# The output phase of an attention layer: where the sync engine packs a chunk's softmax denominators

## The chip, the cores and the metric

The kernel runs on one core of one Trainium2 chip. The metric is the device time of one execution in microseconds (us). The kernel before was timed three times: median 5889.22 us, from 5888.39 to 5891.15.

## The reference

The program is one layer of a convolution-like two-dimensional recurrence, one layer of Nystrom attention and one recurrent feed-forward layer over 16 images of 64 x 64 positions with 128 channels, all in float32. The change lies in the attention layer (8 heads of 16 channels, 64 landmarks), in the part that turns queries into outputs:

```
sim1  = einsum('bhid,bhjd->bhij', q, k_l)       # 4096 queries x 64 landmarks, per head
attn1 = softmax(sim1, axis=-1)
out   = attn1 @ attn2_inv @ (attn3 @ v)          # attn2_inv @ (attn3 @ v) is a small matrix, computed earlier
out   = out + conv1d(v, conv_w)                  # 33 taps along the tokens, per head
out   = x + (out @ w_out + b_out)
```

The result plus the residual is then normalised over the channels of each token and goes to the feed-forward layer.

## The kernel before

The program runs phase after phase: group norm, recurrence, landmarks, pseudo-inverse, output, feed-forward recurrence. The change touches only the output phase, `output_phase`. It works through 16 images (b) of 8 chunks (c) of 512 tokens, so 128 chunks. Every engine has its own program, a loop over the chunks whose body is called `slot(b, c, ...)`; the order in a slot is written out by hand, and semaphores tie the engines together. The engines work on different chunks in one slot (a software pipeline).

What happens to a chunk c:
- TensorE computes its queries (L2138), the maxima's products (L2152), the scores (L2171, L2175), and in `weigh` (L2185) the unnormalised output. ScalarE exponentiates (L2318) and copies the two halves of the heads to the tiles `even` (L2310) and `odd` (L2312); this counts the semaphore `denc`. Each tile holds four heads: of 32 partitions, 16 hold the unnormalised outputs of one head, and the other 16 its softmax denominators, 16 times the same row.
- The sync engine (SP), which here does nothing but issue DMAs, packs the denominators of the 8 heads, one row of 512 each, into the small tile `den_packed` with all 128 partitions in use: `pack(b, c)`, two DMAs from SBUF to SBUF (L1987).
- VectorE merges the halves (`merge`, L2391), waits for the packed denominators and takes their reciprocals (`reciprocals`, L2386), one slot after the chunk's own.
- SP writes the reciprocals to the DRAM scratch `recips` (`spread`, two DMAs, L1996; it waits for the reciprocals, and at L1994 until the broadcast before it has landed, since there is one `recips` for all chunks), and reads them back 16 times each to the tile `rden` (`broadcast`, one DMA of 256 KB, L2003; it waits for the spread to have landed).
- VectorE, a slot later still, waits for `rden`, multiplies (`normalise`, L2397) and adds the convolution (`add_convolved`, L2380, which writes `oT`). TensorE projects `oT` with w_out (`project`, L2211). VectorE adds the residual and takes the statistics (L2366, L2369, L2372), GpSimd (POOL) scales (L2082 to L2089) and SP stores (`store_scaled`, L1978).

So in its slot c VectorE does, in this order: maxima of chunk c+1, residual of c-3, merge and reciprocals of c-1, normalise and add of c-2. SP's slot c is, in this order: store of c-4, load of the base tile c+1 (L1547, waits for the residual of c-3), spread of c-1, the loads of the values `v` (two DMAs of 272 KB, L1553, for the next or next but one image; there are none in the second half of image 14 and in image 15), broadcast of c-1, pack of c, load of the tokens c+6 (L1544). All of them go out on one hardware queue, which is spread over the 16 DMA engines. The values are used by the convolution in TensorE's slot (`convolve`, L2197), which waits for four slots' worth of them at once, at every fourth slot.

Of the kernel before, what the change touches and what calls it, by code (L numbers as in the profile page):

```python
# [1877 lines left out]
def output_phase(nc, sems, R, E, K, xnt, tokens, vals, recips, scaled):  # L1878


    with ExitStack() as ctx:
# [47 lines left out]
        def nth(b, c):  # L1929

            return NG * b + c + 1

        def wait(eng, name, count):

            if count > 0:
                eng.wait_ge(s[name], count)
# [5 lines left out]
        def each_image(eng, slot):  # L1942

            def image(b, q, first, last):
                for c in range(NG):
                    slot(b, c, q, first, last)
            for b in range(B):
                image(b, b % 2, b == 0, b == B - 1)

        def follows(c, k, last):  # L1950

            return c + k < NG or not last

        def precedes(c, k, first):

            return c >= k or not first

        def at(b, c):

            return (b, c) if 0 <= c < NG else (b + c // NG, c % NG)  # L1960
# [3 lines left out]
        @block.sync  # L1964
        def _(sp):
            def load_tokens(b, c):
                E.load_tokens(sp, xnt, b, c)

            def load_base(b, c):
                E.load_base(sp, tokens, b, c)  # L1970

            def load_v(b, half, piece):
                E.load_v(sp, vals, b, half, piece)

            def store_scaled(b, c):
                wait(sp, "u", nth(b, c))
                b0, c0 = at(b, c)
                sp.dma_start(scaled[b0, 512 * c0:512 * c0 + 512, :].rearrange("(n p) c -> p n c", p=P), u[c % 2][:, :, 1:1 + C]  # L1978
                             ).then_inc(s_ust[c % 2], 16)

            def pack(b, c):

                wait(sp, "denc", 2 * nth(b, c))
                wait(sp, "rec", nth(b, c) - 1)
                for h, tile in enumerate((even[c % 2], odd[c % 2])):
                    row = DH * (1 - h)
                    sp.dma_start(den_packed[LM * h:LM * h + LM, :], tile[row:C:QUAD, :].rearrange("g (j e) -> g j e", j=DH)  # L1987
                                 ).then_inc(s_packed, 16)

            def spread(b, c):  # L1990

                wait(sp, "rec", nth(b, c))
                if nth(b, c) > 1:
                    sp.wait_ge(s_rden, 16 * (nth(b, c) - 1))  # L1994
                for h in range(2):
                    sp.dma_start(recips.rearrange("(g a) (j e) -> a g j e", a=2, j=DH)[h], rec_packed[LM * h:LM * h + LM, :]  # L1996
                                 ).then_inc(s_spread, 16)

            def broadcast(b, c):

                sp.wait_ge(s_spread, 32 * nth(b, c))
                wait(sp, "att", nth(b, c) - 2)
                sp.dma_start(rden[c % 2][:, :], recips.unsqueeze(1).broadcast_to([HEADS, DH, 512])).then_inc(s_rden, 16)  # L2003

            def slot(b, c, q, first, last):
                if precedes(c, 4, first):
                    store_scaled(b, c - 4)
                if precedes(c, 3, first) and follows(c, 1, last):
                    wait(sp, "res", nth(b, c - 3))
                    load_base(*at(b, c + 1))  # L2010
                if precedes(c, 1, first):
                    spread(b, c - 1)

                if c < GT and b + 1 < B:
                    wait(sp, "conv", NG * (b + 1))
                    load_v(b + 1, 1, c)
                if c >= GT and b + 2 < B:
                    wait(sp, "conv", NG * (b + 1) + GT)
                    load_v(b + 2, 0, c - GT)
                if precedes(c, 1, first):  # L2020
                    broadcast(b, c - 1)
                pack(b, c)
                if follows(c, 6, last):

                    wait(sp, "qm", nth(b, c + 2))
                    load_tokens(*at(b, c + 6))
            wait(sp, "conv", GT)
            for piece in range(GT):
                load_v(1, 0, piece)
            for c in range(4, 6):  # L2030
                wait(sp, "qm", c - 3)
                load_tokens(0, c)

            each_image(sp, slot)
            spread(B - 1, NG - 1)
            broadcast(B - 1, NG - 1)
            for c in range(NG - 4, NG):
                store_scaled(B - 1, c)
            for q in range(2):
                sp.wait_ge(s_ust[q], 16 * B * NG // 2)  # L2040
# [817 lines left out]
```

## Time and profile before

| | |
|---|---|
| median of three runs | 5889.22 us |
| the profiled execution, its time | 5894.68 us |
| the profiled execution, its span | 5892.9 us |
| mean granted TensorE clock | 0.981 of full speed |
| output phase within the span | about 2520 to 3568 us |
| TensorE busy over the whole span | 89% |
| VectorE, ScalarE, GpSimd busy | 52%, 53%, 26% |

The profile is one execution. Its rows come from several views: groups of busy time, waits (who waited for whom), the timeline (each instruction with its start and its length), and stretches (busy time of each engine between two times). For a DMA, a timeline row is its *issue* on SP's queue, not its transfer; when it landed shows only in what was waiting for it.

### The profile page before, as it was taken

Reading aid. Unit: us, or ns where it says so; the run is one execution under the profiler, and the core shown is the slowest. Engines: PE = TensorE matmul, PEld = TensorE weight load, DVE = VectorE, ACT = ScalarE, POOL = GpSimd, SP = SyncE. Lnnn points to the kernel's source line nnn. Section 1 sums busy time; section 2 is a strip of 40 time slices with the busy share of each in tenths; the row PEclk is TensorE's granted clock in tenths of the full one; section 3 lists DMA queues with packets and bytes.
Section 4 is the critical chain, followed back from the end, with each engine's and each line's share of the span. In section 5 each row is a group of like instructions: output and inputs, shape, how many; then the busy total and the mean of one; then the engine's idle time right before and its main releaser. Section 6 shows DMA issues by size and latency. Waiting matters only on the chain. (4 is left out here: it accounts for less than half of the span.)

```text
span 5892.9 us, 223296 instructions
## 1 busy us (share of the span) xinstructions
PE 5223.6 (89%) x97395; PEld 3271.2 (56%) x97488; DVE 3058.7 (52%) x8152; ACT 3136.4 (53%) x9108; POOL 1516.7 (26%) x1905
## 2 busy tenths in 40 slices
PE   5599999997899888799999997888888888888888
PEld 4599888896566666645555443333333333333333
DVE  8677777775888886568888882111111111111111
ACT  6455555564677776478888883333333333333333
POOL 2100000001888875246666661000000000000000
PEclk7899999999999999999999998999999999999999
DMA  9631111225887773457777762111111111111100
GB/s 389 272 116 58 58 58 58 73 77 183 253 246 236 238 243 116 103 162 207 207 208 207 204 175 66 32 32 32 34 33 32 32 33 34 32 32 32 35 18 24
DMA packets 773031, 689.32 MB, mean 117 GB/s; under 512 B 67056, under 2 KB 663024, under 8 KB 767984
## 3 DMA queue, kind: packets, MB, share of 16 engines
q1 hardware_dynamic: 754672, 575.39, 32.8%
q0 software_dynamic: 14672, 95.16, 4.0%
q8 instruction: 743, 12.17, 0.9%
q10 hardware_dynamic: 2736, 4.89, 0.2%
q14 instruction: 208, 1.70, 0.1%
HBM read 392.17 MB, written 274.89 MB: 113 GB/s over the span
## 5 line engine op out<-in xcount | busy, mean ns | idle before, releaser
L2796 ACT ACTIVATE f_y<-f_acc 128x16 f32<-128x16 f32 x4096 | 753.8, 184 | 1541.3 <-PE f_acc L2738 1541.3
L2738 PEld LDWEIGHTS f_acc<-f_y,f_vT 128*32 128x32 f32 x32768 | 644.8, 108 | 1436.7 <-ACT f_y L2796 1436.1
L2738 PE MATMUL f_acc<-f_y,f_vT 128*32 128x16 f32 x32768 | 1045.7, 193 | 278.1 <-issue 0.4
L2696 PE MATMUL f_junk<-f_idle 128*32 128x512 bf16 x8400 | 831.9, 376 | 0.0
L2578 DVE COPY f_zT<-f_zt 128x512 f32<-128x512 f32 x124 | 85.8, 692 | 1136.6 <-PE f_zt L2652 1136.6
L2355 DVE TENSOR_REDUCE o_m<-o_bank_l 128x8 bf16<-128x512 f32 x512 | 328.8, 683 | 98.7 <-PE o_bank_l L2152 98.7
L2571 DVE TENSOR_SCALAR f_wxn<-f_wxp,f_scale,f_shift 128x512 f32<-128x512 f32 x126 | 102.0, 810 | 508.8 <-PE f_wxp L2666 508.8
L1299 ACT ACTIVATE a_p<-a_s 128x512 f32<-128x512 f32 x502 | 259.2, 602 | 153.6 <-PE a_s L1166 151.7
L533 POOL DMA_DIRECT2D hidden<-l_h x46 | 34.6, 754 | 1162.8 <-DVE l_hsum L790 961.5
L712 ACT ACTIVATE l_gate<-l_pf,r_ctx 128x256 f32<-128x256 f32 (+7 forms) x512 | 202.4, 446 | 229.8 <-PE l_pf L643 229.6
L2318 ACT ACTIVATE o_p<-o_bank_s 128x512 f32<-128x512 f32 x512 | 264.4, 602 | 101.2 <-PE o_bank_s L2175 101.2
L2591 DVE SCALAR_TENSOR_TENSOR f_sum<-f_u,f_std,f_turned 128x128 f32<-128x128 f32 x512 | 143.4, 342 | 317.9 <-PE f_turned L2689 317.9
L2696 PEld LDWEIGHTS f_junk<-f_idle 128*32 128x32 bf16 x8400 | 249.9, 99 | 0.0
L1359 DVE TENSOR_REDUCE a_m3p<-a_s 128x1 f32<-128x512 f32 x360 | 223.4, 682 | 50.0 <-PE a_s L1126 48.5
L633 PE MATMUL l_pio<-l_x,r_k_lm 128*128 128x256 f32 (+7 forms) x1024 | 239.0, 356 | 0.2 <-ACT l_gate L729 0.2
L633 PE MATMUL l_pf<-l_x,r_k_lm 128*128 128x256 f32 (+7 forms) x1024 | 238.9, 356 | 0.0
L647 PE MATMUL l_pio<-l_hsum,r_ctx 128*128 128x256 f32 (+7 forms) x1024 | 238.8, 356 | 0.0
L2302 ACT ACTIVATE o_base<-o_base,r_loss,r_gain 128x128 f32<-128x128 f32 x512 | 225.4, 497 | 0.0
L2689 PE MATMUL f_turned<-f_ident,f_y 128*32 128x128 f32 x4096 | 221.3, 290 | 0.5 <-DVE f_sum L2591 0.5
L1017 POOL TENSOR_TENSOR a_r<-a_vare,a_half 128x8 f32<-128x8 f32 x128 | 209.7, 1639 | 10.0
L712 ACT ACTIVATE l_gate<-l_pio,r_ctx 128x256 f32<-128x256 f32 (+7 forms) x512 | 203.3, 450 | 14.0
L2678 PE MATMUL f_acc<-f_wxn,f_ident 128*32 128x128 f32 x4096 | 207.1, 274 | 0.8 <-issue 0.8
(323 smaller groups left out, 11466.4 us busy)
## 6 DMA issues: line engine op xcount, KB each, us to landing
o_v<-vals SPq DMA_DIRECT2D x256, 272.0 KB
a_hid<-hidden SPq DMA_DIRECT2D x112, 520.0 KB, 5.0
hidden<-l_h POOLq DMA_DIRECT2D x46, 1040.0 KB, 6.8
l_x<-skew SPq DMA_DIRECT2D x46, 1024.0 KB, 5.2
vals<-a_v SPq DMA_DIRECT2D x128, 272.0 KB, 3.6
gn_x<-in_x SPq DMA_DIRECT2D x16, 2048.0 KB, 18.0
a_xin<-in_x SPq DMA_DIRECT2D x128, 256.0 KB, 4.9
tokens<-a_t SPq DMA_DIRECT2D x128, 256.0 KB, 3.4
```

The costliest lines, as they stand in the source:

```text
L633: mm = nc.tensor.matmul(banks[c][g][:, :, rows], w[W[g]], xs, start=g in (0, 2, 3), stop=False, skip_group_check=True)
L647: mm = nc.tensor.matmul(banks[c][g][:, :, rows], w[U[g]], hsum[:, lanes[c], rows], start=False, stop=True, skip_group_check=True)
L712: nc.scalar.activation(gate[:, g, lanes[c], rows], banks[c][g][:, :, rows], ACT.Tanh if g == 2 else ACT.Sigmoid, bias=bias[BI[g]]).then_in ...
L1299: nc.scalar.activation(p3[c % 2][g][:, :], score_bank(i, c, g), ACT.Exp).then_inc(s["exp"], 1)
L1359: nc.vector.tensor_reduce(m3p[:, g, c:c + 1], bank[:, :], AX.X, ALU.max).then_inc(s["mx"], 1)
L2302: nc.scalar.activation(bs[c % 4][:, k, :], bs[c % 4][:, k, :], ACT.Identity, scale=R.gain[:, b, n:n + 1], bias=R.loss[:, b, n:n + 1]).then ...
L2318: nc.scalar.activation(p1[g][:, :], bank_s[g][:, :], ACT.Exp).then_inc(s["exp"], 1)
L2355: nc.vector.tensor_reduce(m1[:, 2 * r:2 * r + 2, LM * half:LM * half + LM].rearrange("p k (g r) -> p k g r", r=QUAD)[:, :, :, 0:2], bank_l ...
L2689: mt = nc.tensor.matmul(turned[g % 2][rows, b % 4, :], y[q][:, rows, b], ident[:, :], start=True, stop=True)
L2696: nc.tensor.matmul(junk[rows, :], idle[:, 0:QUAD], idle[:, :], start=True, stop=True)
L2738: mm = nc.tensor.matmul(acc[k % 2][rows, t, :], vT[:, rows], before, start=False, stop=True, skip_group_check=True)
L2796: nc.scalar.activation(y[q][:, step, :], acc[step // RC % 2][:, step % RC, :], ACT.Sigmoid).then_inc(s_y, 1)
```

## The change

One line moves in SP's slot: `pack(b, c)` now stands directly behind `spread(b, c - 1)`, before the loads of v and before `broadcast(b, c - 1)`.

```diff
@@ -2010,7 +2010,7 @@
                     load_base(*at(b, c + 1))
                 if precedes(c, 1, first):
                     spread(b, c - 1)
-
+                pack(b, c)
                 if c < GT and b + 1 < B:
                     wait(sp, "conv", NG * (b + 1))
                     load_v(b + 1, 1, c)
@@ -2019,7 +2019,6 @@
                     load_v(b + 2, 0, c - GT)
                 if precedes(c, 1, first):
                     broadcast(b, c - 1)
-                pack(b, c)
                 if follows(c, 6, last):
 
                     wait(sp, "qm", nth(b, c + 2))
```

In the body of the phase, SP's instructions of one slot stand like this in the kernel before (recips<-o_rec_packed is the spread, o_v<-vals the values, o_rden<-recips the broadcast, o_den_packed the pack, o_xnT the tokens, scaled<-o_u the store, o_base<-tokens the base tile):

```order
L1996 DMA recips<-o_rec_packed 4x16x32 x2
L1553 DMA o_v<-vals 128x4x136 x2
L2003 DMA o_rden<-recips 128x1x512
L1987 DMA o_den_packed<-o_even 64x1x32
L1987 DMA o_den_packed<-o_odd 64x1x32
L1544 DMA o_xnT<-xnt 128x512
L1978 DMA scaled<-o_u 128x4x128
L1547 DMA o_base<-tokens 128x4x128
```

The same slot in the changed kernel:

```order
L1996 DMA recips<-o_rec_packed 4x16x32 x2
L1987 DMA o_den_packed<-o_even 64x1x32
L1987 DMA o_den_packed<-o_odd 64x1x32
L1553 DMA o_v<-vals 128x4x136 x2
L2003 DMA o_rden<-recips 128x1x512
L1544 DMA o_xnT<-xnt 128x512
L1978 DMA scaled<-o_u 128x4x128
L1547 DMA o_base<-tokens 128x4x128
```

The two small DMAs of the pack have moved ahead of three large ones, and the two values loads and the broadcast have each moved two instructions back. In the last image and a half, where no values are loaded, SP's slot in the changed kernel is:

```order
L1996 DMA recips<-o_rec_packed 4x16x32 x2
L1987 DMA o_den_packed<-o_even 64x1x32
L1987 DMA o_den_packed<-o_odd 64x1x32
L2003 DMA o_rden<-recips 128x1x512
L1544 DMA o_xnT<-xnt 128x512
L1978 DMA scaled<-o_u 128x4x128
L1547 DMA o_base<-tokens 128x4x128
```

There the pack and the broadcast have changed places. The other engines' programs are the same.

## Rows read from the trace of the kernel before

**Rows 1.** Busy time by stretch, output phase while values are still loaded.

```profile
core 0: us, PE busy (x) PEld busy (x) DVE busy (x) ACT busy (x) POOL busy (x), PEclk, DMA share, GB/s
2571.00:3462.00 891.00, 855.33 (x10454) 445.34 (x10454) 739.53 (x1889) 751.25 (x1558) 604.01 (x613) 1.00 0.74 207
```

**Rows 2.** One line of the kernel, L2386 (the reciprocals), same stretch.

```profile
L2386 DVE RECIPROCAL o_rec_packed<-o_den_packed x112: 342/353/355, 2571.5 to 3461.6; 128x32 f32<-128x32 f32 x112
```

**Rows 3.** Waits, same stretch, TensorE: in total us, times, longest.

```profile
PE o_bank_x L2211 <- DVE o_oT L2380: 23.3, 27, 2.4
PE o_bank_s L2197 <- DMA o_v<-vals: 6.8, 8, 1.3
```

**Rows 4.** Waits, same stretch, VectorE.

```profile
DVE o_rec_packed L2386 <- DMA o_den_packed<-o_odd: 56.5, 80, 1.8
DVE o_att L2397 <- DMA o_rden<-recips: 4.7, 6, 1.2
```

**Rows 5.** Waits, same stretch, SP's queue.

```profile
SPq L1994 <- DMA o_rden<-recips: 100.3, 93, 2.1
SPq L1996 <- DVE o_rec_packed L2386: 69.2, 99, 1.8
SPq L2003 <- DMA recips<-o_rec_packed: 11.0, 22, 1.4
```

**Rows 6.** Timeline of SP over one slot: start, length, DMA issued.

```profile
3011.47 1.14 SPq L1996 DMA_DIRECT2D recips<-o_rec_packed  x2
3012.66 1.01 SPq L1553 DMA_DIRECT2D o_v<-vals  x2
3013.85 0.63 SPq L2003 DMA_DIRECT2D o_rden<-recips  x1
3014.58 0.56 SPq L1987 DMA_DIRECT2D o_den_packed<-o_even  x1
3015.19 0.54 SPq L1987 DMA_DIRECT2D o_den_packed<-o_odd  x1
3015.78 0.45 SPq L1544 DMA_DIRECT2D o_xnT<-xnt  x1
...
3019.56 1.15 SPq L1996 DMA_DIRECT2D recips<-o_rec_packed  x2
```

**Rows 7.** SP's waits between 3017.67 and 3019.60 us.

```profile
SPq L1996 <- DVE o_rec_packed L2386: 0.7, 1, 0.7
SPq L1994 <- DMA o_rden<-recips: 0.6, 1, 0.6
```

**Rows 8.** Timeline of VectorE and ScalarE at the end of that slot.

```profile
3017.51 0.59 ACT L2312 ACTIVATE o_odd<-o_bank_s 128x512 f32<-128x512 f32 x1
...
3018.29 0.72 DVE L2391 SCALAR_TENSOR_TENSOR o_att<-o_odd,o_keep,o_pvs 128x512 f32<-128x512 f32 x1
3019.18 0.35 DVE L2386 RECIPROCAL o_rec_packed<-o_den_packed 128x32 f32<-128x32 f32 x1 [0.17 <-DMA o_den_packed<-o_odd]
3019.45 0.63 DVE L2397 TENSOR_TENSOR o_att<-o_att,o_rden 128x512 f32<-128x512 f32 x1
```

**Rows 9.** Timeline of TensorE in that slot, projection, convolution, next projection.

```profile
3013.60 1.16 PE L2211 MATMUL o_bank_x<-o_wo,o_oT 128*128 128x128 f32 x8 [1.21 <-DVE o_oT L2380]
...
3018.12 1.11 PE L2197 MATMUL o_bank_s<-o_v,o_bands 128*64 128x256 f32 x8
...
3021.26 1.16 PE L2211 MATMUL o_bank_x<-o_wo,o_oT 128*128 128x128 f32 x8
```

**Rows 10.** Timeline, one slot earlier: VectorE's normalise beside GpSimd.

```profile
3011.24 1.04 POOL L2089 TENSOR_TENSOR o_u<-o_t,k_rstd 128x512 f32<-128x512 f32 x1
3011.36 1.47 DVE L2397 TENSOR_TENSOR o_att<-o_att,o_rden 128x512 f32<-128x512 f32 x1
...
3012.86 0.69 DVE L2380 TENSOR_TENSOR o_oT<-o_att,o_bank_x 128x512 f32<-128x512 f32 x1
```

**Rows 11.** A late load of v: SP's issue and the convolution.

```profile
3108.53 1.01 SPq L1553 DMA_DIRECT2D o_v<-vals  x2
...
3114.94 1.11 PE L2197 MATMUL o_bank_s<-o_v,o_bands 128*64 128x256 f32 x8 [1.21 <-DMA o_v<-vals]
```

**Rows 12.** SP in a slot without loads of v: timeline.

```profile
3532.62 0.61 SPq L2003 DMA_DIRECT2D o_rden<-recips  x1
...
3537.47 0.57 SPq L1996 DMA_DIRECT2D recips<-o_rec_packed  x1
```

**Rows 13.** SP's waits between 3532.80 and 3537.50 us.

```profile
SPq L1996 <- DVE o_rec_packed L2386: 1.1, 1, 1.1
```

## The prediction

> **What bounds the kernel now.** I read the stretches first. While values are loaded the output phase has TensorE busy for 855 of 891 us at full granted clock, and the 16 DMA engines for 0.74 of the time [rows 1]: TensorE comes near to being the bound, and the DMA engines are not full. The line of the reciprocals then gives the rhythm: 112 of them from 2571.5 to 3461.6 us, so 890.1 / 111 = 8.02 us a slot [rows 2]. TensorE's waits come next: 23.3 us for `oT` and 6.8 us for v [rows 3], together 30.1 us or 0.27 us a slot. TensorE would therefore need 8.02 - 0.27 = 7.75 us a slot by itself; the slot shown, from projection to projection with no wait in it, has 3021.26 - 3013.60 = 7.66 [rows 9].
>
> Why is `oT` late? VectorE waits 56.5 us in 80 slots for the packed denominators and hardly for `rden`, 4.7 us [rows 4]. That looks as if the pack were the problem. SP's waits tell more: it waits 100.3 us (93 times) for the broadcast to land before it may overwrite `recips`, and only after that 69.2 us (99 times) for the reciprocals [rows 5]. One slot shows the two side by side: the wait for the reciprocals before the spread at 3019.56 is 0.7 us [rows 6, 7], so `rden` landed at 3018.86, and the denominators let the reciprocals start at 3019.18 [rows 8]. Pack and broadcast, issued one behind the other, land 0.3 us apart. So there are two loops almost equally long, through one queue:
> - spread, v, broadcast, pack, landing of the pack, reciprocals, next spread;
> - spread, v, broadcast, landing of the broadcast, next spread. This one holds no VectorE work at all.
>
> **The change part by part.** Work is neither added nor removed. *The pack.* Its two issues cost SP 1.20 us (3014.58 to 3015.78) [rows 6]. Now they go out 1.19 us behind the start of the spread (3011.47 to 3012.66). Their wait, `denc`, is free at 3018.10 [rows 8], 2.65 us before the new place of that slot's pack (3019.56 + 1.19 = 3020.75), so it holds nothing up. The pack then has the rest of the slot to land, with nothing large in front of it, and VectorE's 56.5 us of waits for it go. That is the gain, and at most the 23.3 us that TensorE waits for `oT` could come of it in this stretch.
>
> *The loads of v and the broadcast* leave 1.20 us later each. Let S be the start of the spread. Before, v is issued at S + 1.19 and the broadcast at S + 2.38 (3013.85) [rows 6]. When does the broadcast land? Over the stretch: a slot of 8.02 us is 1.19 to the issue of v, plus the time from there to the landing, plus SP's wait for the reciprocals, 69.2 / 111 = 0.62 [rows 2, 5]. What is left is 6.21 us from the issue of v to the landing. The slot shown gives 3018.86 - 3012.66 = 6.20 [rows 6, 7]. A small part of the 6.21 is SP's wait for the spread to land, 11.0 / 111 = 0.10 us [rows 5]; with the pack in between, the spread has 1.20 us longer and this wait mostly goes. I take 6.15. The trace shows no broadcast with 1.20 us of other issues ahead of v, so both ends: below, it could take as little as in a slot without v, where it landed at 3537.47 - 1.1 = 3536.37, that is 3.75 us behind its issue [rows 12, 13], which with 1.19 for v's issues makes 4.94; above, the tokens, the store and the base tile, now issued right behind the broadcast instead of behind the pack, could share the DRAM with it, for which I allow the size that the wait for v shows once (below), 6.41. The likely value stays 6.15, the stretch's own mean, since v and broadcast follow each other as before.
>
> *The new rhythm.* Now the broadcast lands at S + 1.19 + 1.20 + 6.15 = S + 8.54, and the next spread can't start before. The reciprocals no longer add to it: merge ends 0.17 us before the old start of the reciprocals in the slot shown [rows 8], and in the new rhythm far sooner, because TensorE's part of the slot takes 7.7. The slot becomes 8.54 instead of 8.02: the change puts 1.20 into the loop and takes out 0.62 and, with the wait for the spread, 0.06. 0.52 x 112 slots with v = **+58 us**. TensorE then waits some 0.8 us a slot for `oT`, and VectorE for `rden`.
>
> *v itself.* At every fourth slot the convolution needs the v that was issued in the slot before. The trace has one case in which it came late: issued at 3108.53, convolution at 3114.94, so 6.41 us [rows 11]. In the new rhythm the normalise starts with the spread, the projection follows by 1.45 (0.63, 0.69 and hand-overs) [rows 8, 10], the convolution 4.52 after it (3013.60 to 3018.12) [rows 9], at S + 6.0, whereas v lands at S + 2.39 + 5.4 to 6.4, 1.8 to 2.8 us later. Most of this falls into the 0.8 us that TensorE has over in the slot and into the slack of the merge: with projection 3.14 behind the convolution (3018.12 to 3021.26), and merge ending 3019.01 - 3013.60 = 5.41 behind a projection [rows 8, 9], merge ends at S + 16.3 to 17.3, and the spread after next is due at S + 17.1 and needs it 0.4 before. Cost 0 to 0.6 us at 28 places; I take **+8 us**, range 0 to 17.
>
> *The last twelve slots,* without v: the broadcast leaves where it did, behind two small issues instead of two issues of v, lands 3.75 us later [rows 12, 13], long before it is needed, and the pack is early. This gains what VectorE waits there, a few tenths a slot: **-3 us**.
>
> *The normalise* now starts whenever `rden` lands, which may be while GpSimd is at work. In the slot shown it took 1.47 instead of 0.63 us: it began at 3011.36, GpSimd's scaling ran from 3011.24 to 3012.28, and 3012.83 is 0.55 behind that end [rows 8, 10]. "SBUF — State Buffer" of the Trainium skill (its reading of the engine-port diagram) says why: a VectorE instruction with two SBUF inputs and a GpSimd instruction lock a shared port pair for a whole instruction each. The trace agrees, 0.84 us for this one. By this rule a collision delays `oT` and the projection, but neither the spread nor the broadcast hangs on the normalise, and the merge has 8.54 - 1.45 - 5.41 = 1.7 us of slack, so 0.84 costs nothing unless it meets a late v; that is in the range.
>
> Sum: 58 + 8 - 3 = +63 us. Against the profiled execution that is 5894.68 + 63 = 5958; this execution was 5.5 us above the median of its kernel, so I forecast 5889 + 63 = **5952 us**, slower by 1.1%.
>
> **The rivals.**
> 1. *The pack was the real limit.* If the broadcast keeps landing when it did, only the waits for the pack go: TensorE's 23.3 us and some of the end: 5889 - 25 = 5864. For it speaks that VectorE waits 80 times for the pack and 6 times for the broadcast. Against it: the two land 0.3 us apart, and SP's own wait of 100.3 us is for the broadcast. It would need the landing to come 0.8 us sooner than 6.15 us behind the issue of v.
> 2. *The broadcast lands sooner in an emptier queue.* v now starts when the previous slot's loads have had 1.2 us more to drain. If the landing came at 5.6 instead of 6.15, the slot would be 8.02 again: 5889, within the uncertainty. The slot without v with its 3.75 us speaks for it [rows 12, 13], the slot shown, with nothing unusual and 6.20, against it. "DMA: Bandwidth & Descriptors" of the Trainium skill (Latency and other measured facts) puts the fixed part of a DMA down to DRAM latency that shrinks with lighter load, which would push this way; the rows do not separate this part from the transfer.
> 3. *Slower still: v becomes the bound at image boundaries.* If v lands at the upper end and the normalise meets GpSimd's lock as well (0.84), the merge passes its slack at all 28 places by 0.6 + 0.84: 28 x 1.44 = 40 instead of 8, 5984. It decides once v lands more than about 5.9 us behind its issue.
> 4. *The pack waits for `denc`* and holds v and broadcast further: no sign, with 2.65 us to spare.
>
> **How the numbers follow.** Forecast 0.72, rival 1 0.06, rival 2 0.09, rival 3 (with 4) 0.13. A measurement of this kernel can tell 0.2% (12 us) from no change. Faster 0.06, same 0.08 (most of rival 2), slower 0.86. The forecast's own range: the landing 0.25 us sooner or later is 28 us, v 0 to 17: 5920 to 5985. It leaves out rivals 1 and 2 and takes in most of 3; for the range I take 5915 to 5990.
>
> **What would show it.** The slot in the profile after should be 8.5 us where v is loaded and about 7.4 in the last twelve slots. VectorE's waits for `den_packed` should all but vanish and its waits for `rden` grow from 4.7 to some 80 us or more. SP's wait at L1994 should be followed by hardly any wait for the reciprocals (69.2 us before). TensorE's waits for `oT` should go from 23 to about 80 us and those for v from 7 to 30 or more. v and broadcast should stand at S + 2.4 and S + 3.6. I am wrong if the broadcast lands less than 5.6 us behind the issue of v, or if SP still waits for the reciprocals in most slots.

## The result and the profile after

The changed kernel takes 6008.24 us in the median of four runs (6002.44 to 6014.00), the kernel before 5888.81 in four. The ratio is 1.0202, with a 95% interval of 1.0189 to 1.0214: 2.0% slower, +119 us. The direction came as forecast, the loop that sets the slot as well; the size is nearly double (+63 forecast), and the time lies outside the range of 5915 to 5990. The profiled execution took 6014.0 us, with a span of 6011.4.

The line of the reciprocals, in the stretch in which values are loaded (answers to [rows 2]; the line's number is one lower after the change):

```profile
L2385 DVE RECIPROCAL o_rec_packed<-o_den_packed x111: 342/346/349, 2582.7 to 3579.0; 128x32 f32<-128x32 f32 x111
```

(3579.0 - 2582.7) / 110 = 9.06 us a slot, against 8.02. So 111 slots cost some 115 us more; the first slots bring 3 more (the first spread of this stretch is at 2574.85, before at 2571.87).

The waits of SP's queue, of VectorE and of TensorE, 2575 to 3581 us, beside [rows 3 to 5]:

```profile
SPq L1994 <- DMA o_rden<-recips: 304.2, 110, 4.1
SPq L1547 <- DVE o_t L2365: 35.9, 54, 2.4
SPq L1996 <- DVE o_rec_packed L2385: 4.2, 6, 1.4
```
```profile
DVE o_att L2396 <- DMA o_rden<-recips: 148.9, 104, 3.0
```
```profile
PE o_bank_x L2210 <- DVE o_oT L2379: 108.6, 82, 2.5
PE o_bank_s L2196 <- DMA o_v<-vals: 22.9, 17, 2.3
```

VectorE no longer waits for the packed denominators at all: no such row is left. In its place it waits 148.9 us for the broadcast (4.7 before). SP waits three times as long as before for the broadcast to land, 304.2 us, and then hardly ever for the reciprocals, 4.2 us against 69.2. TensorE's wait for `oT` has gone from 23.3 to 108.6 us. The slot is now the second loop alone: spread, broadcast, landing, spread.

One slot of SP in the timeline (start, length, DMA issued), to be read beside [rows 6]:

```profile
3291.16 1.15 SPq L1996 DMA_DIRECT2D recips<-o_rec_packed  x2
3292.41 0.62 SPq L1987 DMA_DIRECT2D o_den_packed<-o_even  x1
3293.07 0.56 SPq L1987 DMA_DIRECT2D o_den_packed<-o_odd  x1
3293.67 1.01 SPq L1553 DMA_DIRECT2D o_v<-vals  x2
3294.78 0.61 SPq L2003 DMA_DIRECT2D o_rden<-recips  x1
3295.44 0.46 SPq L1544 DMA_DIRECT2D o_xnT<-xnt  x1
3295.94 0.43 SPq L1978 DMA_DIRECT2D scaled<-o_u  x1
3296.63 0.36 SPq L1547 DMA_DIRECT2D o_base<-tokens  x1
3300.19 0.56 SPq L1996 DMA_DIRECT2D recips<-o_rec_packed  x1
```

(The last row ends with the stretch that was asked for; the spread has two issues as before.) And VectorE in the same slot:

```profile
3297.88 0.72 DVE L2390 SCALAR_TENSOR_TENSOR o_att<-o_odd,o_keep,o_pvs 128x512 f32<-128x512 f32 x1
3298.52 0.35 DVE L2385 RECIPROCAL o_rec_packed<-o_den_packed 128x32 f32<-128x32 f32 x1
3300.22 1.20 DVE L2396 TENSOR_TENSOR o_att<-o_att,o_rden 128x512 f32<-128x512 f32 x1 [1.36 <-DMA o_rden<-recips]
```

The reciprocals are ready at 3298.87, but the next spread goes out at 3300.19, together with the normalise: both were waiting for the same landing. The broadcast leaves 3.62 us behind the spread (2.38 in the slot of [rows 6]) and lands 3300.19 - 3294.78 = 5.41 us behind its issue. In [rows 6, 7] it was 3018.86 - 3013.85 = 5.01. One more thing differs: the tokens follow the broadcast after 0.66 us, where they stood 1.93 behind it.

Over the stretch the DMA engines are busy for 0.68 of the time (0.74 before). The granted TensorE clock is 0.98 on average (1.00 before): in 10 of the 111 slots (one before) it stands at its lower level, 1.2 GHz, for a part of the slot. The first of these times, at 2648.02, comes 1.22 us behind the end of a wait of TensorE for v of 2.07 us. The ten slots take 9.26 us on average and the rest 9.05, so the clock accounts for some 2 us in all and is not the cause.

In the last slots, where no values are loaded, two starts of the spread in the timeline:

```profile
3649.81 1.16 SPq L1996 DMA_DIRECT2D recips<-o_rec_packed  x2
...
3652.34 0.60 SPq L2003 DMA_DIRECT2D o_rden<-recips  x1
...
3657.12 1.16 SPq L1996 DMA_DIRECT2D recips<-o_rec_packed  x2
```

7.31 us here. Over the twelve slots it is 7.34 on average (7.49 before), a gain of 1.8 us.

### The profile page after: what moved, and what is told of

Its sections match the earlier page's. It is cut to its first block and busy times, and to the rows that moved or that the text cites. A ratio compares the mean times of both kernels' runs of the same rounds, so it can differ in the third digit from the quotient of the medians.

```text
span 6011.4 us, 223389 instructions
## 1 busy us (share of the span) xinstructions
PE 5249.7 (87%) x97488; PEld 3281.5 (55%) x97488; DVE 3092.8 (51%) x8152; ACT 3133.6 (52%) x9108; POOL 1539.1 (26%) x1905
## 5 line engine op out<-in xcount | busy, mean ns | idle before, releaser
L2210 PE MATMUL o_bank_x<-o_wo,o_oT 128*128 128x128 f32 x1024 | 154.0, 295 | 118.6 <-DVE o_oT L2379 118.1
L2210 PEld LDWEIGHTS o_bank_x<-o_wo,o_oT 128*128 128x128 f32 x1024 | 128.9, 197 | 221.1 <-DVE o_oT L2379 218.6
```

The costliest lines, as they stand in the source:

```text
L2210: mt = nc.tensor.matmul(bank_x[:, k, :], oT[:, P * k:P * k + P], wo[:, :], start=True, stop=True)
```

## The experiments

All figures below are for the stretch with values. *Slot* is the spacing of the reciprocals. *Landing* is counted from the broadcast's issue: the slot, less the time from the spread to the issue, less SP's mean wait for the reciprocals. *From v* counts the same landing from the first issue of v. The issue times are means over the slots' timeline rows, from the start of the spread. Ratios are to the kernel before on the same chip. The *followers* are the DMAs issued behind the broadcast: tokens, store and base tile, 256 KB each.

| kernel | ratio (95%) | slot | v issued | broadcast issued | landing | from v |
|---|---|---|---|---|---|---|
| before | 1 | 8.02 | 1.20 | 2.61 | 4.79 | 6.20 |
| changed | 1.0202 (1.0189 to 1.0214) | 9.06 | 2.48 | 3.65 | 5.37 | 6.54 |
| idle DMAs behind the broadcast | 1.0122 (1.0105 to 1.0139) | 8.71 | 2.48 | 3.65 | 4.99 | 6.16 |
| before, idle DMAs in front | 1.0219 (1.0202 to 1.0236) | 9.13 | 2.42 | 3.58 | 4.93 | 6.09 |
| changed, small loads | 1.0123 (1.0109 to 1.0138) | 8.64 | 2.47 | 3.64 | 4.92 | 6.09 |
| before, small loads | 0.9971 (0.9959 to 0.9982) | 7.83 | 1.20 | 2.57 | 4.52 | 5.89 |
| idle DMAs and small loads | 1.0062 (1.0045 to 1.0079) | 8.37 | 2.48 | 3.64 | 4.65 | 5.81 |
| v, pack, broadcast | 1.0043 (1.0029 to 1.0057) | 8.27 | 1.20 | 3.76 | 4.46 | 7.02 |

The landings of this table are worked out from slots and waits. The trace also times the last update of the broadcast's semaphore. By that the mean landing is 4.70 before, 5.31 in the changed kernel and 4.92 with the idle DMAs behind: up to 0.1 us sooner, with nearly the same differences.

### Was it the followers? Two idle DMAs behind the broadcast

`pack_nothing` issues two DMAs of the pack's shape, from a constant tile to a spare one that nothing reads. They put the followers back to where they stood, counted from the broadcast.

```diff
                 if precedes(c, 1, first):
                     broadcast(b, c - 1)
+                pack_nothing(b, c)
```

> The changed kernel with two small DMAs more in each of SP's slots, directly behind the broadcast, where the pack stood before: they copy a constant tile to a spare one (same shapes as the pack; nothing reads it). In the changed kernel the broadcast leaves 3.65 us behind the spread, as forecast (3.57), but lands 5.41 us behind its issue instead of 4.8. Theory A (the followers crowd it): the tokens, the store and the base tile, 768 KB, now start 0.66 us behind the broadcast instead of 1.94, and take engine and DRAM time from its transfer. The two idle DMAs restore the 1.94: it lands 4.8 to 4.9 behind its issue, the slot is 8.5 us, the time about 5950 us. Theory B (what stands ahead of it, the small descriptors of the pack in front of v, slows v and the broadcast): nothing changes, slot 9.07 or a little more, 6008 us or more.

Measured: 5971.59 us, ratio 1.0122, slot 8.71. The reciprocals, and SP's waits, 2575 to 3543 us:

```profile
L2398 DVE RECIPROCAL o_rec_packed<-o_den_packed x111: 342/345/350, 2582.8 to 3541.0; 128x32 f32<-128x32 f32 x111
```
```profile
SPq L2005 <- DMA o_rden<-recips: 149.6, 109, 2.6
SPq L2007 <- DVE o_rec_packed L2398: 7.8, 10, 1.8
```

More instructions, and 0.35 us a slot faster than the changed kernel: the wait for the landing has halved, partly because SP has 1.17 us more to issue before it waits. Counted from v the landing is back at 6.16, close to the 6.20 of the kernel before. Theory B, which foresaw no change, has fallen. The slot is not 8.5, since the landing is 4.99 and not 4.8 to 4.9 behind the issue, and SP still waits 0.07 us a slot for the reciprocals.

The profile also has the followers' own landings, for the tokens in the kernel before, the changed kernel and this one (the last figure: median us from issue to landing):

```profile
o_xnT<-xnt SPq DMA_DIRECT2D x111, 256.0 KB, 3.6
o_xnT<-xnt SPq DMA_DIRECT2D x111, 256.0 KB, 5.2
o_xnT<-xnt SPq DMA_DIRECT2D x111, 256.0 KB, 3.8
```

Issued right behind the broadcast the tokens take 5.2 us instead of 3.6, and the store and the base tile 5.4 and 5.5 instead of 3.9 and 4.1. With the idle DMAs between they are back at 3.8, 4.1 and 4.3. So the followers, too, take longer for standing close.

### The other way round: two idle DMAs in the kernel before, in front of v

```diff
                 if precedes(c, 1, first):
                     spread(b, c - 1)
-
+                pack_nothing(b, c)
```

> The kernel before with the same two idle small DMAs put between the spread and the loads of v; the real pack stays behind the broadcast, so the broadcast's followers keep their distance. Theory A (followers): the broadcast leaves at 3.6 us and lands 4.8 behind that, the packed denominators 0.3 later, reciprocals, next spread 0.7 behind the landing: slot 9.1 us, about 6010 us. Theory B (what stands ahead): it lands 5.4 behind its issue, slot 9.7, about 6080 us. Rival of both (issue time in front of v costs nothing, the forecast's first rival): slot 8.0, 5889 us.

Measured: 6026.3 us, ratio 1.0219, slot 9.13, where theory A had 9.1 and theory B 9.7. Here the packed denominators land last, so VectorE waits for them, 2576 to 3590 us:

```profile
DVE o_rec_packed L2398 <- DMA o_den_packed<-o_odd: 156.6, 106, 2.9
```

1.2 us of issue time ahead of v costs 1.1 us a slot, nearly all of it. Two small DMAs ahead do not slow the transfer itself: it lands 6.09 behind v's issue (6.20 before).

### Breaking the loop: two buffers for the reciprocals, in both kernels

```diff
-                if nth(b, c) > 1:
-                    sp.wait_ge(s_rden, 16 * (nth(b, c) - 1))
+                if nth(b, c) > 2:
+                    sp.wait_ge(s_rden[c % 2], 16 * ((nth(b, c) - 1) // 2))
...
-    recips = scratch("recips", (HEADS, 512))
+    recips = [scratch(f"recips{k}", (HEADS, 512)) for k in range(2)]
```

In the changed kernel:

> The changed kernel with two DRAM buffers for the reciprocals, so that a spread waits for the broadcast two chunks back and not for the last. Loop theory (the slot is spread, broadcast, landing, next spread): the spread goes out right behind the reciprocals; the normalise still waits for the landing, some 9.07 us behind its spread, but projection, residual and merge behind it take about 7.2 us and then two slots have passed: (9.07 + 7.2) / 2 = 8.1 to 8.3 us a slot, 5900 to 5925 us. Rival (the DMA queue itself is too slow for the order, whatever SP waits for): slot 9.07, 6008 us.

Measured: 5944.1 us, ratio 1.0076 (1.0059 to 1.0092), slot 8.49. The loop theory's direction holds and its rival (9.07) falls: the queue can go faster once SP need not wait for the last landing. The value is above the 8.1 to 8.3 expected. TensorE still waits 52.3 us for `oT` and 25.8 for v. The second half of my sum had left out the late v, the longer normalise (919 ns on average) and SP's wait for the residual ahead of the spread (91.4 us); which of them makes the difference was not tried.

In the kernel before:

> The kernel before with two DRAM buffers for the reciprocals, nothing else. If in the kernel before the loop through the pack (spread, v, broadcast, pack, its landing, reciprocals, next spread) is the longer of the two, nothing changes: slot 8.0, within 0.2%. If the wait for the broadcast's landing is what sets the rhythm there too, it gets faster, to about TensorE's 7.75 a slot, 0.5%.

Measured: 5890.53 us, ratio 1.0001 (0.9992 to 1.0010), slot 7.99. SP's waits for the landing are gone and have become waits for the reciprocals, 2578 to 3465 us, beside [rows 5]:

```profile
SPq L1996 <- DVE o_rec_packed L2386: 162.0, 108, 3.7
SPq L2003 <- DMA recips<-o_rec_packed: 12.0, 26, 1.0
```

162.0 is nearly what the two were together (100.3 + 69.2 = 169.5). So in the kernel before the loop through the pack set the rhythm, and SP's 100.3 us for the broadcast cost nothing measurable, although it was the longest wait on the queue.

### Half of the change: v, pack, broadcast

```diff
                     load_v(b + 2, 0, c - GT)
+                pack(b, c)
                 if precedes(c, 1, first):
                     broadcast(b, c - 1)
-                pack(b, c)
```

> Half of the change: the pack stands behind the loads of v and ahead of the broadcast. v leaves as in the kernel before (1.19 us behind the spread), the broadcast as in the changed one (3.6), the tokens 0.66 us behind it. If the landing is counted from v (v's transfer holds the broadcast up, theory B or plain first-in-first-out): it lands 6.15 behind v, slot 7.8 to 8.0, 5875 to 5890 us. Theory A (the followers crowd the broadcast): 4.8 to 5.0 behind its issue, slot 8.5, 5945 us.

Measured: 5924.16 us, ratio 1.0043, slot 8.27, between the two expectations. The broadcast lands 4.46 behind its issue and 7.02 behind v's: neither is constant by itself. Its followers stand as close as in the changed kernel (0.65 us), yet it lands 0.91 sooner behind its issue (4.46 for 5.37), while v stands 2.56 us ahead of it and not 1.17: what goes out shortly before the broadcast counts as well as what follows it. v, early again, costs TensorE 1.5 us of waits instead of 22.9. Leaving v in its place thus brings back 0.8 of the 1.04 us that the whole change costs a slot.

### Is it the followers' bytes? Smaller loads in both kernels

From the second image on these kernels load only a part of the tokens and of the base tile, 352 KB of followers instead of 768, and so leave out part of the data.

```diff
-                E.load_tokens(sp, xnt, b, c)
+                if b == 0:
+                    E.load_tokens(sp, xnt, b, c)
+                else:
+                    sp.dma_start(E.xnT[c % 4][:, 0:64], xnt[b, :, 512 * c:512 * c + 64]).then_inc(E.s_xl[c % 4], 16)
...
-                E.load_base(sp, tokens, b, c)
+                if b == 0:
+                    E.load_base(sp, tokens, b, c)
+                else:
+                    sp.dma_start(E.bs[c % 4][:, 0:1, :], tokens[b, 512 * c:512 * c + P, :].rearrange("(n p) c -> p n c", p=P)
+                                 ).then_inc(E.s_bl[c % 4], 16)
```

> The changed kernel with the two loads behind the broadcast cut in size, from the second image on: the tokens to 64 of 512 columns, the base tile to one of its four rows of tiles; this leaves out part of the data, the instructions and their places are the same. Followers by size: 352 instead of 768 KB behind the broadcast, it lands 4.9 to 5.1 behind its issue instead of 5.41, slot 8.55 to 8.75, 5955 to 5975 us beside 6008. If only the issue of DMAs right behind it matters (number and place of instructions, not bytes): 9.07, no change.

Measured: 5963.3 us, ratio 1.0123, slot 8.64. Bytes count: the same instructions in the same places, and the landing is 0.45 sooner. The control:

> The kernel before with the same two loads cut in size (tokens to 64 of 512 columns, base to one of four parts, from the second image on; part of the data is left out). It is the control for the same cut in the changed kernel, where the landing went from 5.4 to 5.0 us and the slot from 9.07 to 8.64. If the followers only crowd the broadcast when they stand right behind it, here, 1.94 us behind, the landing stays at 4.7 to 4.8 and the slot at 7.9 to 8.0: 0 to 0.3% faster. If a queue with less in it is faster whatever the distance: landing 4.4, slot 7.75 (TensorE's bound), 0.5% faster, and the distance explains nothing.

Measured: 5878.15 us, ratio 0.9971, slot 7.83. SP's waits, 2577 to 3447 us:

```profile
SPq L2003 <- DVE o_rec_packed L2393: 83.0, 109, 1.4
SPq L2001 <- DMA o_rden<-recips: 81.5, 90, 1.9
```

The landing came 0.27 us sooner here too, with the loads far behind the broadcast; I had expected 0 to 0.1. The slot lies between the two expectations (7.9 to 8.0, and 7.75). And both together in the changed kernel:

> The changed kernel with both: the two idle small DMAs behind the broadcast and the cut loads (part of the data is left out). If distance and size are two ways to the same thing (crowding), they don't add up: landing 4.9 to 5.0 behind its issue, slot 8.55 to 8.65, as the cut alone (8.64). If they are two separate effects (0.36 and 0.43 us a slot): slot 8.3.

Measured: 5934.08 us, ratio 1.0062, slot 8.37, near the 8.3 of two separate effects and not the 8.6 of one. So "crowding" was too simple. Distance gives 0.35 us with full loads (9.06 to 8.71) and 0.27 with small ones (8.64 to 8.37). Size gives 0.42 when the loads stand close (9.06 to 8.64), 0.34 when they stand off (8.71 to 8.37), and 0.19 of slot, 0.27 of landing, in the kernel before. They are mostly additive.

### A pack outside the loop

With two tiles of packed denominators a pack need not wait for the last reciprocals and can stand ahead of the spread.

```diff
-        den_packed = m.sb("o_den_packed", [P, 512 // DH])
+        den_packed = [m.sb(f"o_den_packed{k}", [P, 512 // DH]) for k in range(2)]
...
-                wait(sp, "rec", nth(b, c) - 1)
+                wait(sp, "rec", nth(b, c) - 2)
...
+                pack(b, c)
                 if precedes(c, 1, first):
                     spread(b, c - 1)
-                pack(b, c)
```

> The pack taken out of the loop altogether: two tiles for the packed denominators, so that a pack need not wait for the reciprocals before it, and the pack stands ahead of the spread, in the time in which SP waits for the broadcast's landing anyway. v and broadcast leave 1.2 and 2.4 us behind the spread as in the kernel before; the tokens follow the broadcast at 0.66 us. Loop theory with crowding followers: landing 2.4 + 5.4 = 7.8 behind the spread, as long as TensorE's own 7.75: slot 7.8 to 7.9, 0.3 to 0.4% faster than before. Loop theory without crowding: 7.3, TensorE bounds at 7.75, 0.5% faster. Rival (the pack only matters by the issue time, and the denominators' lateness was hidden): slot 8.0, same as before.

Measured: 5886.85 us beside 5892.87, ratio 0.9989 (0.9979 to 0.9998), slot (3462.5 - 2584.9) / 110 = 7.98. SP's waits, 2578 to 3464 us:

```profile
SPq L1547 <- DVE o_t L2365: 91.7, 93, 2.7
SPq L1987 <- ACT o_odd L2311: 67.8, 100, 2.0
SPq L2003 <- DMA recips<-o_rec_packed: 32.7, 52, 1.5
SPq L1994 <- DMA o_rden<-recips: 23.2, 29, 2.1
```

The loop through the landing is no longer the bound (23.2 us), and neither is the pack's. But the pack now waits for ScalarE's copy, 67.8 us, and holds the spread behind it; the gain is 0.04 us a slot where 0.1 to 0.2 was expected. With the tokens ahead of the spread as well:

```diff
+                if follows(c, 6, last):
+
+                    wait(sp, "qm", nth(b, c + 2))
+                    load_tokens(*at(b, c + 6))
                 pack(b, c)
                 if precedes(c, 1, first):
                     spread(b, c - 1)
...
-                if follows(c, 6, last):
-
-                    wait(sp, "qm", nth(b, c + 2))
-                    load_tokens(*at(b, c + 6))
```

> As the kernel with two tiles of packed denominators, and the load of the tokens also moved ahead of the spread. Behind the broadcast now only the store and the base tile follow (512 instead of 768 KB), ahead of v there are 256 KB more. Crowding by followers alone: landing 7.5 to 7.8 behind the spread, slot 7.75 to 7.8, 0.4 to 0.5% faster than before. If what stands ahead counts as much: v and broadcast land up to 0.9 later, slot 8.2 or more, slower than before.

Measured: 5883.1 us, ratio 0.9984 (0.9975 to 0.9993), slot (3441.7 - 2579.3) / 110 = 7.84. TensorE's waits, 2573 to 3443 us:

```profile
PE o_bank_x L2210 <- DVE o_oT L2379: 11.0, 13, 1.3
PE o_bank_s L2196 <- DMA o_v<-vals: 1.9, 2, 1.0
```

12.9 us of waits are left of the 30.1 in [rows 3]; without them the slot is 7.84 - 0.12 = 7.72, TensorE's own time. The expected 7.75 to 7.8 and 0.4 to 0.5% were not reached: the gain is 0.16%, and the execution profiled here (5874.18 us) was 9 us faster than the median, so the usual slot is nearer to 7.9. It has the lowest ratio of the kernels that leave nothing out, though not clear of the 0.9989 before it.

## Why the prediction was right in kind and wrong in size

**What held.** That two loops of nearly equal length run through SP: shown by SP's wait for the landing, which with two buffers became a wait for the reciprocals at an unchanged time. That 1.20 us of issue time ahead of v and the broadcast goes into the loop: shown by the idle DMAs in front, +1.1 us a slot. That the wait for the reciprocals (0.62 us a slot) leaves it: 0.04 is left. That v comes late at some places and that this falls into slack: TensorE's waits for it are 22.9 us in 17 slots ("30 or more" expected), and SP waited only 4.2 us for reciprocals, so the late v reached the spread hardly at all. The 8 us that I had set for it were nearly nothing. They went by a landing 5.4 to 6.4 us behind v's issue; in the changed kernel the median is 3.3 and the latest 5.7:

```profile
o_v<-vals SPq DMA_DIRECT2D x222, 272.0 KB, 3.3
```

That the last twelve slots gain: 1.8 us, 3 forecast. That the pack never waits for `denc`.

**What failed** is one step: "The likely value stays 6.15, the stretch's own mean, since v and broadcast follow each other as before." The landing was 6.54 behind v's issue, beyond even the upper bound of 6.41. v and broadcast do follow each other as before; what had moved was what follows *them*. I had named it (the tokens, the store and the base tile "now issued right behind the broadcast") and gave it an allowance in the range, sized by one late load of v that had nothing to do with it, instead of a place in the sum. With the followers held off again (1.83 us behind the broadcast, 0.66 in the changed kernel), the landing is 6.16, my number. So this term of the sum was too small by 0.39 us; x 111 slots that is 43 us.

The rest is small: v left 2.48 and not 2.39 us behind the spread, 0.09 x 111 = 10 us, in part since the pack starts 0.10 us behind the end of the spread (3291.16 + 1.15 = 3292.31, the pack at 3292.41), where v started 0.05 behind it in [rows 6], in part since its two issues took 1.26 us (3292.41 to 3293.67) and not 1.20; 0.04 us of waits for the reciprocals, 4 us; the first slots, 3 us. Together: slots 9.06 - 8.02 = 1.04, of which 0.52 were forecast and 0.39 + 0.09 + 0.04 were not. With v's 8 us taken out and the last slots' 1 us less gain that makes 63 + 43 + 10 + 4 + 3 - 8 + 1 = 116 of the 119 us. The forecast's own range adds up to 5916 to 5989 (28 us for the landing, 0 to 17 for v) and not 5920 to 5985; the range of 5915 to 5990 covers it.

**The rivals.** The first (the pack as the real limit) had half a truth: in the kernel before, the pack's loop was the longer one, which the two buffers showed (1.0001). But the other lay right under it, and the broadcast did not keep landing when it did. The second foresaw a landing sooner in an emptier queue. It came later, although each slot carried the same bytes in more time; yet that fewer bytes land sooner is real (0.27 us with the small loads). The third had the nearest time, 5984, by luck: its reason did not come about. The normalise did take longer, 1048 ns on average instead of 728, but SP hardly waited for the reciprocals behind it (4.2 us), so that did not set the slot. The fourth (the pack waits for `denc`) left no row in SP's waits.

**Left open.** Which of the followers does it, the reads from DRAM or the store, and whether they share an engine's time or the memory's, was not tried. Nor is it known why smaller loads help even 1.9 us behind the broadcast. One thing in the traces was not followed up: they hold nine updates of the broadcast's semaphore per transfer (1152 for 128 in the kernel before) and sixteen for the tokens (512 for 32). The broadcast, whose outermost dimension is the 8 heads, may thus be spread over only half of the 16 DMA engines; no run tries a form that uses more.

## What to carry to other kernels

On a queue whose loop is "issue, land, issue again", count for every moved instruction not only what it puts ahead of the critical transfer but also what it lets close up behind it: here v left 1.28 us later, the slot grew by 1.04, and holding the followers off again gave 0.35 back. When two waits sit side by side and one is hidden under the other, work out the second loop's length before removing the first. A small transfer that many wait for gains little by going first if it pushes a large one that is as late; taking it out of the loop (a second buffer) costs nothing, though here it gave only 0.1 to 0.2%.

## What the runs showed of the hardware

- Two small DMAs *added* behind a 256 KB broadcast made a kernel 0.8% faster (1.0202 to 1.0122): the 768 KB behind it started 1.17 us later, and the broadcast landed 0.38 us sooner. With fewer bytes in the same places (352 KB) it landed 0.45 us sooner. So here DMAs issued later on the same queue delayed one issued earlier. "DMA: Bandwidth & Descriptors" of the Trainium skill (Two DMAs through the same engine are not ordered) says that descriptors start in order but are pipelined, with separate read and write sides. The runs agree as far as they go; a queue that finished each transfer before it began the next would not have shown this.
- VectorE's normalise again ended 0.55 us behind GpSimd's overlapping instruction in the slot shown, as in [rows 10]: GpSimd's scaling ran to 3300.87, the normalise to 3301.42.

```profile
3299.83 1.04 POOL L2088 TENSOR_TENSOR o_u<-o_t,k_rstd 128x512 f32<-128x512 f32 x1
```
